# Edge tensor products of an attention layer rebuilt from signed planes

## The reference

```python
msg_s = (s_n @ Ws_src)[src] + (s_n @ Ws_dst)[dst]
msg_v = (v_n . Wv_src)[src] + (v_n . Wv_dst)[dst]
y0, y1 = (rsh[:, 0], rsh[:, 1:4])
w1 = rbf @ W_rbf                       # 224 radial weights for each edge
m1_s, m1_v = _cg_tp(msg_s, msg_v, y0, y1, *split(w1))
a = sum(leaky(m1_s @ W_alpha) * alpha_dot)                # the logits
val_s, val_v = m1_s @ Ws_val, m1_v . Wv_val
val_v, val_s = val_v * sigmoid(val_s @ Wg), sigmoid(val_s)
m2_s, m2_v = _cg_tp(val_s, val_v, y0, y1, *w2)
hs, hv = m2_s @ Ws_vlin, m2_v . Wv_vlin

def _cg_tp(s, v, y0, y1, w_ss, w_sv, w_vs, w_vv0, w_vv1):
    out_s = concat([w_ss * s * y0, w_vv0 * dot(v, y1) / SQRT3])
    out_v = concat([(w_sv * s) * y1, w_vs * v * y0, w_vv1 * cross(v, y1) / SQRT2])
```

## Time and profile before

| | |
|---|---|
| median of 3 runs | 6455.58 us (6455.34 to 6458.41) |
| the profiled execution | 6450.41 us, its span 6448.6 us |
| busy: PE, DVE, POOL, ACT | 75%, 75%, 66%, 36% |
| L1242, once for each of the 202 groups, starts | 1280.0 to 3664.5 us |
| granted TensorE clock over the program | 0.886 |

### The profile page before, as it was taken

The page is one execution under the profiler, slowest core; times in us unless marked ns, Lnnn a source line. Parts: engine busy times, 40 slices in busy tenths (PEclk is TensorE's granted clock), DMA queues, the critical chain, the costliest instruction groups (busy, mean ns, idle before and its releaser), DMA issues. The chain is left out here.

```text
span 6448.6 us, 162454 instructions
## 1 busy us (share of the span) xinstructions
PE 4844.0 (75%) x45499; PEld 3772.4 (58%) x45500; DVE 4815.1 (75%) x10999; ACT 2313.8 (36%) x6999; POOL 4226.7 (66%) x4249
## 2 busy tenths in 40 slices
PE   6666767388888888888888769876666677777775
PEld 3444445277777777777777757644444454444444
DVE  5777776488888898888888764577777756666665
ACT  1000002266666666666666567410000020000011
POOL 5777775177767777777777347277777727777771
PEclk8888888699999999999999989888888887777777
DMA  3333332133333333333333247222222212222221
GB/s 107 92 93 92 92 92 69 42 90 94 92 89 92 89 92 92 90 92 91 90 92 89 67 148 229 62 73 73 72 72 72 72 40 70 69 69 69 69 69 35
DMA packets 401394, 545.14 MB, mean 85 GB/s; under 512 B 144934, under 2 KB 283318, under 8 KB 401180
## 3 DMA queue, kind: packets, MB, share of 16 engines
q0 software_dynamic: 193920, 331.22, 21.0%
q1 hardware_dynamic: 207388, 212.84, 11.3%
HBM read 464.79 MB, written 78.90 MB: 84 GB/s over the span
## 5 line engine op out<-in xcount | busy, mean ns | idle before, releaser
L805 POOL DMA_INDIRECT e_rows<-tab,e_idx x2424 | 2291.2, 945 | 811.0 <-issue 690.4
L1074 POOL DMA_INDIRECT acc<-tabx,a_idx x1616 | 1686.5, 1044 | 869.9 <-issue 467.9
L850 PE MATMUL e_wps<-e_w,e_hidT 64*128 64x192 f32 (+1 forms) x4848 | 790.6, 460 | 874.6 <-DVE e_hidT L921 871.5
L850 PEld LDWEIGHTS e_wps<-e_w,e_hidT 64*128 64x128 f32 x4848 | 538.2, 250 | 1079.1 <-DVE e_hidT L921 965.4
L835 PE MATMUL e_win<-e_feat,e_ohy 128*32 128x96 f32 (+1 forms) x19392 | 1025.6, 330 | 27.1 <-DVE e_feat L915 25.6
L835 PEld LDWEIGHTS e_win<-e_feat,e_ohy 128*32 128x32 f32 x19392 | 707.2, 131 | 455.9 <-issue 293.9
L906 DVE TENSOR_TENSOR e_feat<-e_wps,e_rows 128x256 f32<-128x256 f32 x606 | 257.5, 425 | 834.5 <-DMA e_rows<-tab,e_idx 761.2
L915 DVE TENSOR_TENSOR e_feat<-e_wps,e_rows 128x384 f32<-128x384 f32 (+1 forms) x1616 | 720.5, 498 | 0.0
L1137 PE MATMUL a_c<-acc,a_buffer 128*128 128x64 f32 (+1 forms) x4848 | 624.9, 272 | 121.6 <-ACT a_buffer L1115 121.6
L824 ACT ACTIVATE e_idx<-src 128x4 int32 (+1 forms) x606 | 123.2, 204 | 1606.4 <-DMA e_rows<-tab,e_idx 1585.1
L1137 PEld LDWEIGHTS a_c<-acc,a_buffer 128*128 128x128 f32 (+1 forms) x4848 | 590.5, 192 | 143.6 <-issue 143.6
(11 more groups left out here) (252 smaller groups left out, 7851.2 us busy)
## 6 DMA issues: line engine op xcount, KB each, us to landing
h_d<-a_buffer SPq DMA_DIRECT2D x202, 322.0 KB, 2.5
s_hin<-h_d SPq DMA_DIRECT2D x202, 322.0 KB, 3.5
e_rows<-tab,e_idx POOLq DMA_INDIRECT x2424
e_ein<-in_e64T SPq DMA_DIRECT2D x202, 128.0 KB
acc<-tabx,a_idx POOLq DMA_INDIRECT x1616
a_ein<-in_e_h SPq DMA_DIRECT2D x202, 64.0 KB
e_ein<-in_e16T SPq DMA_DIRECT2D x202, 32.0 KB
tab<-p_rows SPq DMA_DIRECT2D x36, 160.0 KB
```

What stands on the lines that cost most here:

```text
L805: pool.indirect_dma_start(out=rows[:, s, t, :], out_offset=None, in_=k.tab0, in_offset=bass.IndirectOffsetOnAxis(ap=idx[:, s, t:t + 1], ax ...
L850: mm = pe.matmul(wps[:, e, 2 * u + j, 0:WC], hidT[half, edges], w2[half, :], start=True, stop=True)
L1074: pool.indirect_dma_start(out=rows[:, b, q, :], out_offset=None, in_=table, in_offset=bass.IndirectOffsetOnAxis(ap=idx[:, b, end, q:q + 1] ...
```

## The change

The ten numbers of an edge become thirteen: y1 in an order in which planes 0 to 3 minus planes 4 to 7 of the nine give the first two terms of the dot product (with one sign turned by ScalarE, new L1107) and the three components of the cross product, plain y1 in places 9 to 11, and y0 in place 12. In `head` one subtraction of 512 columns makes all four, and one addition of 128 columns completes the dot product. In `mid` two subtractions write into z directly, and one addition follows. The products with y0 (L1110) are written over the radial weights in PSUM instead of into `wy`, so that one multiplication (new L1247) does both products with the scalars. The rows of two weight matrices trade places to suit the new order in z. The diff is cut to the instructions; the host side only reorders columns of the inputs, and the other uses of y0 and y1 read the new places.

```diff
-        ybuf = scratch(U, TPG, 10)
+        ybuf = scratch(U, TPG, 13)
-        wy = scratch(TPG, 96)
-        vy, red, cr = scratch(TPG, 3, 3, V), scratch(TPG, V), scratch(TPG, 3, V)
+        vy, dc = scratch(TPG, 3, 3, V), scratch(TPG, 4, V)
@@ ScalarE
                         hold(act, k, y_in[b], uses(s, i, 2) * 16 + 16)
+                        act.activation(ybuf[:, b, :, 4], ybuf[:, b, :, 4], ACT.Copy, scale=-1.0)
                         hold(act, k, w_ready, g + 3)
                         for q in range(TPG):
-                            ins = act.activation(wy[:, q, :], wps[:, q, 0:96], ACT.Copy, scale=ybuf[:, b, q, 9:10])
+                            ins = act.activation(wps[:, q, 0:96], wps[:, q, 0:96], ACT.Copy, scale=ybuf[:, b, q, 12:13])
@@ VectorE
-                def cross(to, of, signal):
-                    v.tensor_tensor(to[:, :, 1:3, :], of[:, :, 1, ::-2, :], of[:, :, 2, 0:2, :], ALU.subtract).then_inc(signal, 1)
-                    v.tensor_tensor(to[:, :, 0:1, :], of[:, :, 1, 1:2, :], of[:, :, 2, 2:3, :], ALU.subtract).then_inc(signal, 1)
+                def turned_planes(of):
+                    return of.rearrange("p t j x c -> p t (j x) c")
@@ head
                     hold(v, k, head_ops, at + 1)
-                    v.tensor_tensor(feat[:, :, 0:S], wy[:, :, 0:S], m[:, :, 0:S], ALU.mult).then_inc(head_ops, 1)
+                    v.tensor_tensor(feat[:, :, 0:192].rearrange("p t (o c) -> p t o c", o=2)[:, :, :, 0:S],
+                                    wps[:, :, 0:192].rearrange("p t (o c) -> p t o c", o=2)[:, :, :, 0:S],
+                                    over(m[:, :, 0:S], 2, 2), ALU.mult).then_inc(head_ops, 1)
                     with_planes(vy, mv, y).then_inc(head_ops, 1)
-                    v.tensor_tensor(feat[:, :, 96:160], wps[:, :, 96:160], m[:, :, 0:S], ALU.mult).then_inc(head_ops, 1)
+                    v.tensor_tensor(pair[:, :, :, 0:V], over(wps[:, :, S:96], 2, 3), mv, ALU.mult).then_inc(head_ops, 1)
                     hold(v, k, head_ops, at + 3)
-                    v.tensor_reduce(red[:, :, :], vy[:, :, 0, :, :].rearrange("p t x c -> p t c x"), AX.X, ALU.add).then_inc(head_ops, 1)
-                    v.tensor_tensor(pair[:, :, :, 0:V], over(wy[:, :, S:96], 2, 3), mv, ALU.mult).then_inc(head_ops, 1)
-                    cross(cr, vy, head_ops)
+                    of = turned_planes(vy)
+                    v.tensor_tensor(dc[:, :, :, :], of[:, :, 0:4, :], of[:, :, 4:8, :], ALU.subtract).then_inc(head_ops, 1)
                     hold(v, k, head_ops, at + 5)
-                    v.tensor_tensor(feat[:, :, S:96], wps[:, :, 160:192], red[:, :, :], ALU.mult).then_inc(head_ops, 1)
-                    hold(v, k, head_ops, at + 8)
-                    v.tensor_tensor(pair[:, :, :, V:2 * V], over(wps[:, :, 192:224], 2, 3), cr[:, :, :, :], ALU.mult).then_inc(head_ops, 1)
+                    v.tensor_tensor(pair[:, :, :, V:2 * V], over(wps[:, :, 192:224], 2, 3), dc[:, :, 1:4, :], ALU.mult).then_inc(head_ops, 1)
+                    v.tensor_tensor(dc[:, :, 0, :], dc[:, :, 0, :], of[:, :, 8, :], ALU.add).then_inc(head_ops, 1)
+                    hold(v, k, head_ops, at + 7)
+                    v.tensor_tensor(feat[:, :, S:96], wps[:, :, 160:192], dc[:, :, 0, :], ALU.mult).then_inc(head_ops, 1)
@@ mid
-                    v.tensor_reduce(zz[:, :, S:96], ty[:, :, 0, :, :].rearrange("p t x c -> p t c x"), AX.X, ALU.add).then_inc(mid_ops, 1)
-                    cross(pair[:, :, :, V:2 * V], ty, mid_ops)
+                    of = turned_planes(ty)
+                    v.tensor_tensor(zz[:, :, 2 * V:8 * V].rearrange("p t (u w) -> p t u w", u=2)[:, :, :, 0:V], of[:, :, 0:2, :],
+                                    of[:, :, 4:6, :], ALU.subtract).then_inc(mid_ops, 1)
+                    v.tensor_tensor(zz[:, :, 7 * V:11 * V].rearrange("p t (u w) -> p t u w", u=2)[:, :, :, 0:V], of[:, :, 2:4, :],
+                                    of[:, :, 6:8, :], ALU.subtract).then_inc(mid_ops, 1)
+                    hold(v, k, mid_ops, at + 7)
+                    v.tensor_tensor(zz[:, :, S:96], zz[:, :, S:96], of[:, :, 8, :], ALU.add).then_inc(mid_ops, 1)
```

More of the change, by code:

```diff
@@ L959, in attention_logits @@
     U = 4
-    HEAD, MID, TAIL = 10, 9, 2
+    HEAD, MID, TAIL = 8, 9, 2
     with ExitStack() as scope:
@@ L1058, in step @@
                         sp.dma_start(ybuf[:, b, :, :].rearrange("p t y -> p (t y)"),
-                                     a["y10_t"][bass.ds(g + 3, 1), :, :].rearrange("o p c -> p (o c)")).then_inc(y_in[b], 16)
+                                     a["y13_t"][bass.ds(g + 3, 1), :, :].rearrange("o p c -> p (o c)")).then_inc(y_in[b], 16)
                 rounds(sp, n, step, before=5, after=1, lo=U, U=U)
@@ L1101, in step @@
                         for q in range(TPG):
-                            ins = act.activation(z[:, s % 2, q, 160:352].rearrange("p (x w) -> p x w", x=3)[:, :, 0:V], vec[:, q, :, :],
-                                                 ACT.Copy, scale=ybuf[:, s, q, 9:10])
+                            ins = act.activation(z[:, s % 2, q, 160:352].rearrange("p (x w) -> p x w", x=3)[:, :, V:2 * V], vec[:, q, :, :],
+                                                 ACT.Copy, scale=ybuf[:, s, q, 12:13])
                         ins.then_inc(vy_ready, 1)
@@ L1123, in step @@
                         for q in range(TPG):
-                            ins = act.activation(z[:, o, q, 0:S], z[:, o, q, 96:160], ACT.Copy, scale=ybuf[:, (s + 1) % U, q, 9:10])
+                            ins = act.activation(z[:, o, q, 0:S], z[:, o, q, 96:160], ACT.Copy, scale=ybuf[:, (s + 1) % U, q, 12:13])
                         ins.then_inc(sy_ready, 1)
@@ L1215, in _ @@
                 alpha = cw["L1_c0"][:, S:2 * S].rearrange("p (q c) -> p q c", q=H)
-                leak = red[0:96, :, 0:16]
+                leak = dc[0:96, :, 0, 0:16]
                 wchain.link(v.tensor_tensor(leak, alpha, adot[0:96, :].rearrange("p (q c) -> p q c", q=H), ALU.mult))
@@ L1262, in mid @@
                     zz = z[:, s % 2, :, :]
-                    pair = zz[:, :, 160:352].rearrange("p t (x w) -> p t x w", x=3)
                     at = g * MID
@@ L1266, in mid @@
                     hold(v, k, sig_ready, g + 1)
-                    v.tensor_tensor(t[:, :, :, :], over(fv[:, :, 0:V], 2, 3), planes(y, 0), ALU.mult).then_inc(mid_ops, 1)
+                    v.tensor_tensor(t[:, :, :, :], over(fv[:, :, 0:V], 2, 3), planes(y, 9), ALU.mult).then_inc(mid_ops, 1)
                     v.tensor_tensor(lk[:, s % 2, :, :, 0:16], rect[:, s % 2, :, :].rearrange("p t (q c) -> p t q c", q=H),
@@ L1292, in tail @@
                     v.wait_ge(hs_ready, g + 1)
-                    v.tensor_tensor(t5[:, :, :, :], over(c2[:, :, S:96], 2, 3), planes(ybuf[:, s % U, :, :], 0), ALU.mult).then_inc(tail_ops, 1)
+                    v.tensor_tensor(t5[:, :, :, :], over(c2[:, :, S:96], 2, 3), planes(ybuf[:, s % U, :, :], 9), ALU.mult).then_inc(tail_ops, 1)
                     if not isinstance(g, int) or g >= 2:
@@ L1870, in _arrays @@
         "e64T": edge(i["edge_attr_64"]).T, "e16T": edge(i["edge_attr_16"]).T, "e8T": edge(i["edge_attr_8"]).T,
-        "y10_t": edge(i["edge_attr_4"]).reshape(G, TPG, P, 4)[..., [1, 2, 3, 2, 3, 1, 3, 1, 2, 0]].transpose(0, 2, 1, 3).reshape(G, P, TPG * 10),
+        "y13_t": edge(i["edge_attr_4"]).reshape(G, TPG, P, 4)[..., [1, 3, 1, 2, 2, 2, 3, 1, 3, 1, 2, 3, 0]].transpose(0, 2, 1, 3).reshape(G, P, TPG * 13),
         "ends_t": np.stack([edge(src).reshape(G, TPG, P), edge(dst, fill=N).reshape(G, TPG, P)], 1).transpose(0, 3, 1, 2).reshape(G, P, 2 * TPG),
@@ L1950, in _arrays @@
     a["L1_c3_c"] = const((96, 64), [(0, 0, (64, 64), 1), (64, 0, (32, 64), r3)])
+    riap = lambda r, c, m: [(r, c, m[2]), (r + V, c, m[1])]
     for name, m in (("L1_c4", three), ("L1_c4_f", factors), ("L1_c4_c", bent(three))):
-        a[name] = _place((P, 64), [(0, 0, m[0])] + pair(64, 32, m))
+        a[name] = _place((P, 64), [(0, 0, m[0])] + riap(64, 32, m))
     for name, m in (("L1_c5", three), ("L1_c5_f", factors), ("L1_c5_c", bent(three))):
-        a[name] = _place((P, 64), pair(0, 0, m) + pair(64, 32, m))
+        a[name] = _place((P, 64), riap(0, 0, m) + riap(64, 32, m))
     w = np.zeros((P, SLOTS, D), f)
```

## The result

The changed kernel takes 6465.5 us (median of 20 runs, 6461.2 to 6472.0), the kernel before 6456.7 us on the same chip (20 runs, 6451.7 to 6464.7). The ratio is 1.0014, with a 95% interval of 1.0008 to 1.0020. That is inside the 0.2% called "no change", and inside the range. Yet the interval lies clear of 1: 8.8 us were lost, where the forecast had none.

A forecast was written before the change was run, and what follows sets the result against it. The ring of TensorE and ScalarE was taken as the bound at 11.84 us a round; VectorE's 11.54 (11.64 + 0.06 - 0.16) and ScalarE's 0.11 stay hidden, so 0 us change: forecast 6456 us, range 6438 to 6484.

The forecast's parts named there:

- The ring: TensorE and ScalarE, alternating through the single transpose tile, set the round of 11.84 us; VectorE has about 0.2 us to spare.
- The head: VectorE, L1248 to L1267 before: 4.23 us becomes 4.29, as two new waits at 0.23 outweigh 0.40 saved.
- Mid: VectorE, L1285 to L1293 before: 1.04 us becomes 0.88, saving 0.16 a round.
- ScalarE: Inside the ring, added L1107 costs 0.11 us, hidden in 0.16 of room before L1115; L1110 into PSUM keeps 0.23 a step.
- The failed step: End of VectorE's sum: nobody waits for the head sooner than the transposes, as gathers run four groups ahead; priced at nothing.
- rival 2: VectorE becomes the bound through costlier waits in head and ahead of L1267: 57 us at worst, typically 6476 us; chance 0.09.
- the 13 us bound: Whole program: about 0.2%, 13 us, is what a measurement can tell from no change; "same" was given 0.68.
- the share of "slower": Whole program: chance 0.2 of a slower kernel, from ScalarE's addition stretching the ring (0.16) and VectorE becoming the bound (0.09).

The follow-up runs named there:

- TensorE's waits alone: Kernel before, with the wait that ends last put last in two of TensorE's rows of three waits: 6391.4 us, ratio 0.9900 at full clock.
- the halves: Changed kernel with each VectorE product with planes (L1226, 1152 columns) issued as two of 576: 6454.3 us, ratio 1.0000 to the kernel before.
- the seven gathers: Seven gathers a group instead of eight, part of the output left out: changed kernel 6453.8 us, ratio 1.0002; kernel before with the same edit 6455.4, ratio 0.9999.
- head and mid alone: Kernel before with only the new head, 9475.4 us, ratio 0.9960, or only the new mid, 9421.9 us, ratio 0.9901; both at the low clock.

## Why the prediction was right, and where it was not

**The ring sets the pace: right.** TensorE's waits alone gave 62.8 us with VectorE's code unchanged, and for ninety groups the changed kernel keeps 11.84 with 0.3 us less VectorE busy time a round (forecast about 0.4). The saving was hidden, as forecast.

**The head: right.** L1247 to L1267 is 2717.02 - 2712.69 = 4.33 us, forecast 4.29. The idle time ahead of L1256 is 2715.86 - 2715.71 = 0.15, and ahead of L1259 2716.76 - 2716.62 = 0.14: the two new waits cost the 0.23 each that the earlier trace rows had for L1297. (Ahead of L1297 stand two holds and not a single one as the prediction has it, but the one for L1293's result is the last of them.) While the lead lasts, the head ends 0.50 to 0.62 us ahead of the transposes, against 0.65 to 0.81 before; the prediction allowed for a loss down to 0.3. **Mid: right.** L1286 to L1298 is 0.88, forecast 0.88.

**ScalarE: right.** L1115 still starts 0.13 behind its transpose, which runs from 2710.82 to 2711.42, and L1110's block ends 2.64 us behind the start of the third copy (2708.93), against 2.56 in the earlier trace rows, so 0.1 later as forecast. Its timeline, after:

```profile
2709.43 1.16 ACT L1101 ACTIVATE a_buffer<-acc 128x96 f32<-128x96 f32 x4
2710.49 0.20 ACT L1107 ACTIVATE acc<-acc 128x4 f32<-128x4 f32 x1
2710.59 0.98 ACT L1110 ACTIVATE a_wps<-a_wps,acc 128x96 f32<-128x96 f32 x4
2711.55 0.59 ACT L1115 ACTIVATE a_buffer<-a_tps 96x512 f32<-96x512 f32 x1
```

L1107 puts 0.10 us between its start and the next, forecast 0.11. L1110 into PSUM takes 0.98 for four against 1.01: a single one is 0.03 shorter (the row's median is 306 ns, x808, against a mean of 334 in the earlier trace rows), the step of 0.23 is the same. Leaving L1107 out gained nothing.

```profile
L1110 ACT ACTIVATE a_wps<-a_wps,acc x808: 288/306/322, 1276.7 to 3674.7; 128x96 f32<-128x96 f32 x162
```

The Trainium skill, ScalarE: Activation LUTs, section Step-by-step: what each stage is for, has it that ScalarE's way to PSUM is faster than that to SBUF. The trace agrees by 0.03 us for one activation, and shows nothing of it in the step between two.

**The failed step.** It stands at the end of VectorE's sum: "nobody else waits for it sooner, as the gathers run four groups ahead". Priced at nothing, it cost 0.05 to 0.06 us a round in the second half, 5.3 of the 7.5 us by which the stage grew. Before the change the lead was real, 30.4 us. But a lead is a stock and not a cover: it says nothing on whether the gathers keep the pace, and with the new order of VectorE it did not even build up. The earlier trace rows had it in view: GpSimd was busy for 493 of 700 us, 8.3 us a round with 8 x 0.30 between gathers on top, 10.7 of 11.84. The gathers' lengths, 0.95 us here and 1.44 there, were not looked at, and their cause was VectorE's instructions, the very ones that the change moves. What is shown is the hold (by the timelines) and its part in the loss (by the halves and the seven gathers). That the loss comes from the new distances between the two products with planes is argued from the timelines, and not tried: with head and mid alone no answer came. From the start of head's product to that of mid's it was 6.31 us and is 6.18, from mid's to the next head's it was 5.53 and is 5.66 (means of groups 40 to 90; the 5.84 from 2707.46 to 2713.30 in the round shown holds a wait for gathers).

One sign that the prediction named as wrong did come, transposes 0.15 behind the head's end in the second half. It was given to rival 2, in which VectorE's own waits are too long. The seven gathers take it away with VectorE's code as it was, so here it is a sign of the gathers.

So the main mechanism was right, and the number held in part by luck: the missed term was small against the 13 us bound, and the share of "slower" in the forecast stood for other mechanisms than the one that came.

## What to carry to other kernels

Find the bound by the engine whose instruction comes back evenly, and test it by shortening that ring alone; a busy share of 90% was not the bound here. Price an engine that runs ahead by its time a round against the round, including what others do to it, not by its lead: when VectorE's long instructions move, look at the lengths of GpSimd's gathers as well. In a row of waits, put the one that ends last at the end: here two swaps on TensorE, whose waits were in the ring, were worth 1%, seven times what the change cost.

## What the runs showed of the hardware

- A gather issued while a 1.35 us product with both inputs in SBUF runs on VectorE ends 0.81 to 0.83 us after that product, so it takes up to 2.1 us instead of 0.95. Behind the first addition (0.82 us, both inputs in SBUF) it takes up to 1.60. One that started first is not slowed (0.94), nor is one that starts up to 0.03 us after the product; in that case the product is the one that gets longer, by up to 0.07 us (1422 ns against a median of 1349; 30 of 404 are over 1355).
- Waits that are already met are not free when they stand behind the one that ends last: TensorE sat idle for 0.60 us a round ahead of `a_c` with two of them behind, and 0.20 with none, and ahead of `a_scal` 0.64 and 0.28, so about 0.2 each (a wait with its increment).
- On two chips the same programs ran at a granted clock of 0.66 in this stage (0.68 over the whole program, where others had 0.88 to 0.89), and the kernel before took about 9500 us. The ranking of the kernels there was another one, so results from them were not used for the causes.
